# Post-LN transformer layer on eight cores: V jobs moved four blocks, part of the output projection inside head 15, bias on VectorE, one load of constants

## The reference

```
q = (x @ Wq.T + bq) * cos(rot);  k = (x @ Wk.T + bk) * sin(rot);  v = x @ Wv.T + bv     # by head
scores = q @ k.T / sqrt(128) * spiral_weight[head]
attn_out = concat_heads(softmax(scores) @ v) @ Wo.T + bo
x = layernorm(x + attn_out)
h = gelu(x @ proj1.T + proj1_bias)        # 8192 wide, exact gelu
out = layernorm(x + h @ proj2.T + proj2_bias)
```

## Time and profile before

| | |
|---|---|
| median of the runs | 1903.7 us |
| the profiled execution | 1906.13 us outside, its slowest core 2 has a span of 1904.7 us |
| spans of the eight cores | 1893.7 to 1904.7 us, clock 0.987 to 0.991 |
| TensorE busy | 1815.4 us (95%) |
| VectorE, ScalarE, GpSimd busy | 677.6, 555.0, 180.3 us (36%, 29%, 9%) |
| chain that ended last | TensorE 90%, DMA 3%, VectorE 3% |
| first matmul | at 24.3 us, after a wait that ended with the load of `spiral_bc` |
| HBM | 240.32 MB read, 18.87 MB written |

### The profile page before, as it was taken

How to read it: one execution, slowest core, us unless ns; L and a number is a source line. 1 busy time by engine, 2 the same in 40 slices (tenths; PEclk the granted TensorE clock), 3 DMA queues, 4 the chain that set the end, 5 groups by cost and what they waited for, 6 DMA issues and landing times.

```text
span 1904.7 us, 22132 instructions; the slowest of 8 cores (1893.7 to 1904.7 us)
## 1 busy us (share of the span) xinstructions
PE 1815.4 (95%) x8344; PEld 821.9 (43%) x8512; DVE 677.6 (36%) x732; ACT 555.0 (29%) x560; POOL 180.3 (9%) x260
## 2 busy tenths in 40 slices
PE   4999999999999999968899999999999999999998
PEld 1444444444444443323444444444444444444443
DVE  0136666666666667786751000000000020120303
ACT  0145555555555556642332111111110000000002
POOL 2000000000000000050220000000000000000001
PEclk9999999999999999978999999999999999999999
DMA  9661014101411123176344444444443465444665
GB/s 150 112 113 23 15 20 72 23 15 20 67 23 23 23 34 55 23 147 119 133 152 103 75 75 75 77 76 77 78 78 67 80 138 100 97 96 87 154 117 171
DMA packets 46039, 151.59 MB, mean 80 GB/s; under 512 B 6128, under 2 KB 6256, under 8 KB 43632
## 3 DMA queue, kind: packets, MB, share of 16 engines
q0 software_dynamic: 29952, 109.07, 34.1%
q1 hardware_dynamic: 15984, 41.10, 6.4%
HBM read 240.32 MB, written 18.87 MB: 136 GB/s over the span
## 4 chain that ended last, share of the span: by engine, by line
PE 90%; DMA 3%; DVE 3%; DVEq 1%; ACT 1%; issue 1%; POOL 0%; ACTq 0%; POOLq 0%
PE ps L674 22%; PE ps L701 22%; PE ps L381 11%; PE ps L389 11%; PE ps L385 6%; PE ps L569 6%; PE ps L532 5%; PE ps L640 3%; DMA W<-wvc 2%; PE ps L601 1%; DMA H<-p2n 1%; DVE X L924 1%; PE ps L652 1%; PE ps L542 1%; DVEq L927 1%
## 5 line engine op out<-in xcount | busy, mean ns | idle before, releaser
L674 PE MATMUL ps<-X,W 128*128 128x512 bf16 x1945 | 426.3, 379 | 2.1
L701 PE MATMUL ps<-W,H 128*128 128x512 bf16 x1882 | 414.2, 379 | 2.0
L776 ACT ACTIVATE X<-ps,neg_b 128x1024 bf16<-128x1024 f32 x256 | 284.2, 1113 | 303.6 <-PE ps L569 283.5
L928 DVE TENSOR_TENSOR X<-X 128x1024 f32<-128x1024 f32 x224 | 274.4, 1225 | 212.7 <-ACT X L776 202.8
L674 PEld LDWEIGHTS ps<-X,W 128*128 128x128 bf16 x1984 | 194.1, 98 | 234.1
L701 PEld LDWEIGHTS ps<-W,H 128*128 128x128 bf16 x1920 | 188.1, 98 | 227.3 <-issue 1.3
L381 PE MATMUL ps<-H,W 128*128 128x512 bf16 x1007 | 254.2, 380 | 25.2 <-DMA spiral_bc<-spiralr 24.3
L985 DVE TENSOR_TENSOR X<-ps,bo_bc 128x512 f32<-128x512 f32 x24 | 16.4, 685 | 685.9 <-PE ps L701 685.5
L389 PE MATMUL ps<-W,H 128*128 128x512 bf16 x1004 | 246.4, 381 | 3.6 <-DMA W<-wvc 1.8
L532 PE MATMUL ps<-X,H 128*128 128x512 bf16 x496 | 153.8, 390 | 25.6 <-ACT X L776 24.0
L828 ACT ACTIVATE H<-ps,b_sb 128x1024 bf16<-128x1024 f32 x64 | 71.2, 1113 | 360.3 <-PE ps L674 359.2
(11 more groups left out here) (92 smaller groups left out, 856.9 us busy)
## 6 DMA issues: line engine op xcount, KB each, us to landing
W<-p1t POOLq DMA_DIRECT2D x64, 512.0 KB, 5.0
W<-p2n POOLq DMA_DIRECT2D x60, 512.0 KB, 6.7
W<-wkt POOLq DMA_DIRECT2D x16, 512.0 KB, 5.1
H<-xtc POOLq DMA_DIRECT2D x16, 512.0 KB, 50.4
W<-wvc POOLq DMA_DIRECT2D x16, 512.0 KB, 14.6
W<-wqt POOLq DMA_DIRECT2D x16, 512.0 KB, 5.1
H<-won POOLq DMA_DIRECT2D x16, 512.0 KB, 17.3
bo_bc<-x_scr SPq DMA_DIRECT2D x32, 256.0 KB, 6.9
```

The lines of the kernel that those rows point to most:

```text
L674: ins = t.matmul(bank[b0 + c], wslab[ring(ho)][:, half(i, 128)], X[:, i * 1024 + c * 512:i * 1024 + (c + 1) * 512], start=(i == 0), stop=( ...
L701: ins = t.matmul(bank[s], hid[k][:, half(s, 128)], w[:, half(i, 512)], start=(k == 0), stop=(k == 63))
L776: a.activation(out=pbuf[n % 3], in_=pair[turn(h, tc) % 2], func=AF.Exp, bias=neg_b[:, h:h + 1]).then_inc(a_exp, 1)
L928: v.tensor_add(acc, acc, pbuf[n % 3]).then_inc(d_acc, 1)
```

## The change

**V.** The lead-in makes 12 of the 16 V blocks of the first four heads. The last four are jobs of head 0, and each round of later V blocks is made four blocks, that is one head, later. `jobs(12)` goes from 6 to 10.

**Steps.** Heads 13 and 14 (6 jobs) get 8 job matmuls a step instead of 10, and their norms move from step 12 to 13 (squares accordingly).

**Output projection.** The weights of heads 4 to 7 go to the V slabs of W, those of 8 to 15 where x chunks 0 and 1 lay; they load in groups of four in heads 13, 14 and 15. In steps 2 to 15 of head 15, TensorE does two of block 1's matmuls (banks 6 and 7) for heads 0 to 13, ahead of the step's P times V. After the head come banks 4 and 5 of block 1, then block 0.

**Bias.** VectorE adds the output bias, in pieces of 512 columns: three blocks before the projection's first bank, then one block ahead, two pieces after bank 2 and two after the scaling. GpSimd's adds are gone. The xn loads wait for step 8 of head 15 as well. Slabs 2 to 5 of the MLP wait for the end of the projection.

**Constants.** Helix, bq, bk, spiral and pick come in one load of 128 x 72; the two arrays of ones are set by VectorE. TensorE no longer waits for them. The loads of gelu bias, identity, output bias and the second V bias wait for 8 V blocks.

```diff
 def jobs(h):
-    return 10 if h < 12 else 6 if h < 15 else 0
+    return 10 if h < 13 else 6 if h < 15 else 0
+def per_step(h):
+    return 10 if h < 13 else 8
+def norm_step(h):
+    return 12 if h < 13 else 13
...
         def _(e):
-            for dst, src in ((helix_sb, helix2), (bk2_sb, bk2), (bq2_sb, bq2),
-                             (ones_sq_sb, ones_sq), (onesf_sb, onesf),
-                             (pick8_sb, pick8)):
-                e.dma_start(out=dst[:], in_=src[:]).then_inc(s_bias, 16)
-            e.dma_start(out=spiral_bc[:], in_=spiralr.to_broadcast([128, 16]),
-                        ).then_inc(s_bias, 16)
+            e.dma_start(out=consts_sb[:], in_=consts[:]).then_inc(s_bias, 16)
             for c in range(4):
-                if c == 2:
+                if c == 1:
+                    e.wait_ge(d_v, 8)
...
             e.wait_ge(pe_q, 32)
-            for s in (2, 0, 1):
+            e.wait_ge(pe_sc, 248)
+            for s in range(3):
                 e.dma_start(out=xb[s], in_=xn[s * 128:(s + 1) * 128, :]).then_inc(s_xb[s], 16)
...
-                if h % 4 == 0 and h < 12:
-                    e.wait_ge(pe_v, 4 * h + 16)
+                if h % 4 == 1 and h < 12:
+                    e.wait_ge(pe_v, 4 * h + 12)
...
+                if h == 13:
+                    e.wait_ge(pe_v, 64)
+                    for d in range(4, 8):
+                        load(wo_sb[d], won[d], s_wo[d])
+                if h == 14:
+                    e.wait_ge(pe_k, 64)
+                    e.wait_ge(pe_q, 32)
+                    for d in range(8, 12):
+                        load(wo_sb[d], won[d], s_wo[d])
-            e.wait_ge(pe_v, 64)
-            e.wait_ge(pe_q, 32)
-            for d in range(4, 16):
+            for d in range(12, 16):
                 load(wo_sb[d], won[d], s_wo[d])
-
-            def add_bo(s):
-                e.wait_ge(s_xb[s % 3], 16 * (s // 3 + 1))
-                e.tensor_add(xb[s % 3], xb[s % 3], bo_bc[:]).then_inc(g_bo, 1)
...
-            t.wait_ge(s_bias, 112)
...
                 else:
-                    ins = v_mm(4 * (h % 4) + j - 6, i, b)
+                    ins = v_mm((12 + 4 * h + j - 6) % 16, i, b)
...
+                if h % 4 == 0 and tc in (0, 12, 13, 14, 15):
+                    t.wait_ge(d_v, 4 * h + max(12, tc + 1))
...
+                    u = per_step(h) * tc
+                    fill(h, u, u + per_step(h) // 2)
+                    if h == 15 and tc >= 2:
+                        if tc == 2:
+                            t.wait_ge(a_q, 32)
+                        wo_ready(tc - 2)
+                        for c in (2, 3):
+                            wo_mm(1, tc - 2, c)
                     if n > 0:
                         p_v(n - 1)
...
+            def add_bo(s, c):
+                if c == 0:
+                    v.wait_ge(s_xb[s % 3], 16 * (s // 3 + 1))
+                v.tensor_add(xb[s % 3][:, half(c, 512)], xb[s % 3][:, half(c, 512)],
+                             bo_bc[:, half(c, 512)])
+
+            v.wait_ge(s_bo, 16)
+            for s in range(3):
+                for c in range(4):
+                    add_bo(s, c)
+            v.drain()
             for s in range(8):
-                v.wait_ge(g_bo, s + 1)
                 for c in range(4):
...
+                    if c == 2 and 2 <= s < 7:
+                        add_bo(s + 1, 0)
+                        add_bo(s + 1, 1)
...
+                if 2 <= s < 7:
+                    add_bo(s + 1, 2)
+                    add_bo(s + 1, 3)
+                    v.drain()
```

More of the change, by code:

```diff
@@ L545, in denom, with wo_ready, wo_mm @@
                 ins.then_inc(pe_den, 1)
+            def wo_ready(d):
+                t.wait_ge(s_wo[d], 16)
+                t.wait_ge(d_norm, d + 1)
+            def wo_mm(s, d, c):
+                ins = t.matmul(bank[s * 4 + c], pool_a[d][:, half(s, 128)],
+                               wo_sb[d][:, half(c, 512)], start=(d == 0), stop=(d == 15))
+                if d == 15:
+                    ins.then_inc(pe_wo, 1)
             for h in range(16):
@@ L596, in transposes @@
                     ins.then_inc(pe_tr, 1)
[L600 to L616 removed]
+            t.wait_ge(a_av, 16)
+            for d in range(8):
+                for c in (0, 1):
+                    wo_mm(1, d, c)
+            t.wait_ge(a_exp, 255)
+            denom(15, pair[(turn(15, 15) + 1) % 2])
+            for d in range(8, 14):
+                for c in (0, 1):
+                    wo_mm(1, d, c)
             t.wait_ge(a_exp, 256)
             t.wait_ge(a_den, 16)
[L619 removed]
+            for d in range(14):
                 for c in range(4):
                     wo_mm(0, d, c)
[L622 to L624 removed]
+            for d in range(14, 16):
+                wo_ready(d)
                 for s in range(2):
@@ L906, in normalise @@
                 v.tensor_mul(pool_a[h], avraw, rec).then_inc(d_norm, 1)
[L908 to L909 removed]
+            for m in range(11):
+                v_out(m, ((2, 3, 4, 5), (0, 2, 3, 1), (5, 4, 4))[m // 4][m % 4])
             norm_pick(0, pair[1])
[L911 removed]
+            v_out(11, 5)
             norm_out(0, pair[1])
[L913 removed]
             for h in range(16):
@@ L932, in _ @@
                         normalise(h - 1)
+                    for j in range(6, jobs(h)):
+                        if tc == (16 * j + 15) // per_step(h):
+                            v_out(6 + 4 * h + j, 6 + j % 2)
                     if tc == 15:
@@ L937, in _ @@
                         v.tensor_sub(hl[:, half(1)], acc, hl[:, half(0)]).then_inc(d_hl, 1)
-                    for j in range(6, jobs(h)):
-                        if tc == (16 * j + 15) // PER_STEP:
-                            v_out(10 + 4 * h + j, 6 + j % 2)
             for i in range(4):
```

187 lines of the change are left out of this document (71 added, 116 removed).

## The result

| | before | after |
|---|---|---|
| runs | 1903.53 us median (1903.34 to 1904.17) | 1877.07 and 1878.39 us |
| profiled execution | 1906.13 us | 1877.07 us |
| span of its slowest core | 1904.7 us (core 2) | 1875.4 us (core 4) |
| spans of all cores | 1893.7 to 1904.7 us | 1866.5 to 1875.4 us |
| TensorE busy | 1815.4 us (95%) | 1809.8 us (97%) |

The ratio is 0.9864, 95% interval 0.984 to 0.9888: 25.9 us less; the forecast, 1870 against 1903.7, was 33.7. Two more runs of the changed kernel fell in a disturbed state with a lower clock (2167 and 2179 us) and are left out, so its time rests on two runs.

A forecast was written before the change was run, and what follows sets the result against it. TensorE, busy in 95% of the span, was taken as the bound. Terms -3.0 + 0.6 - 9.1 - 14.0 - 4.9 - 3.0 = -33.4 took the profiled 1906.1 us to 1872.7, as median 1870; range 1861 to 1881.

The forecast's parts named there:

- A, start: Start of the lead-in: fewer small loads land the last V piece 4.2 us earlier, slow clock costs 1.2; -3.0 us.
- A2, lead-in: Lead-in: loads issued after 8 V blocks cost 0 (bounds 0 to +4.4), with 3.2 us slack for the third K chunk.
- rival 2: Start gains nothing and takes some: broadcasts ahead of x cost +4.4 us, 1875, or 1878 with the slow clock; 12%.
- A3, norm of head 0: End of lead-in: without the 16th V block, head 0's norm is no longer hidden; +0.6 us (0 to 1.2).
- B, V: Four V blocks leave the lead-in (-13.8 us), heads 12 to 14 grow by 4.7; -9.1 us (-13.4 to -5.1).
- C, head 15: Head 15: VectorE's chain without its stall cuts 41.3 us to 27.3, including +1.9 for slow clock; -14.0 (-15.9 to -10).
- Rival 1: Head 15: DMA traffic, not GpSimd, stalls VectorE, so the head's gain shrinks to nothing: 1884 us; 3%.
- D, first projection: Output projection of the first two blocks: 28 matmuls less (-6.0), +0.4 and +1.0 in waits; -4.9 us (-5.9 to -3).
- E, blocks 2 to 7: Projection blocks 2 to 7: no stretched VectorE scalings, the transposes' 3.4 us of waits go; -3.0 us (-3.4 to +2).
- Rival 3: TensorE leaves head 15 at 1.2 GHz and stays there through the projection: up to +104 us, 1975; 2%.
- Rival 4: Weights for head 15's projection matmuls come up to 6 us late and stop TensorE: 1876 us; 5%.
- The 2.4 us to the median: The median of the runs lies 2.4 us below the profiled execution, so the forecast goes from 1872.7 to 1870.

The follow-up runs named there:

- the start alone: Kernel before with one load of constants, memsets, no TensorE wait, identity and gelu bias after 8 V blocks, output bias after 16: ratio 0.9973.
- the best version: Changed kernel with later output-bias load, ScalarE copying block 0's transposes earlier, head 14's reciprocals and normalise behind head 15's sums, GpSimd adding blocks 1-2's bias: 1863.84 us.

## Why the prediction was right, and where not

The time (1877.7 by the ratio, 1877.07 and 1878.39 by its runs) lies in the range of 1861 to 1881 but 7.7 us above the forecast of 1870: the gain was 25.9 us, not 33.4. By parts, from the experiments: -15.6 (bias) - 5.1 (start) - 3.4 (V) - 5.9 (matmuls in head 15) = -30.0, and +3.8 for the output bias that is issued after 8 V blocks, which none of the single parts contains (the start alone issued it after 16). That gives -26.2 against -25.9 measured. So close an agreement is luck, since each part is uncertain by 2 to 5 us; the means of the cores give -25.2 against -26.3. That the early broadcast costs only with V moved is argued, not shown: no run has it without that move. On the means the misses are 2.0 us up to the first scores, 2.9 in heads 12 to 14 and 2.3 in the projection; head 15 came out as forecast (-14.1).

- **A, start: right place, one term wrong.** "Removing that wait is not worth 24 us" is confirmed: it is worth 0. I took -3.0; the mean core gained 4.3 us, the slowest 6.6. The 4.2 us for the small loads was nearly right: on the mean of the eight cores the last V piece starts at 40.4 us before, at 36.1 with the start alone and at 35.6 in the changed kernel. What was wrong is the 1.2 us for the lower level: the last piece's 16 matmuls ran at full rate on all eight cores (3.61 or 3.62 us), and the slow ones were earlier (5.64 us at 16.61), where a wait followed anyway. So the cold start cost 0. The rule of the Trainium skill, "TensorE: Matmul & The Clock Gate", section "HAM oscillation — how this bites in real kernels", which I had weighed at 3.45 us on that piece, did not hold for it; the wait in front of it was 1.75 us, and the waits of the page's example are longer, so this says nothing against the page. In other runs it did happen on single cores, at no cost to the last piece: with the start alone, on core 6, the third piece took 5.30 us behind a wait of 2.12.
- **A2, lead-in: wrong, and the largest miss.** I worked out a slack of 3.2 us and let the broadcast come "mostly behind x". It came beside it: 4.03 us of wait. With the slow matmuls after it, that is rival 2, whose +4.4 was about right (3.8 by the runs; 3.2 in the first scores on the mean core, 5.1 on the last). I gave it 12%. Its own rows spoke for it: 1.3 MB issued at 69 us while x was due at 77 to 80.
- **A3, norm of head 0: right place, cost not there.** First scores follow the norm at once. The first exponent is not waited for: the norm is written at 93.87 us on core 4, and P times V starts at 95.65 without a wait, 4.1 us of matmuls behind the first scores where I had counted 3.0. The +0.6 was 0.
- **B, V: the lead-in part right, the idle time wrong.** Head 12 took 49.25 us, as forecast (49 to 50). Heads 13 and 14 idled 6.3 and 7.0 us; I took 4.5 and 6.0, believing that smaller steps would fill the idle time. Three settings (8, 10 and 12 a step) say that they do not: the norm's waits stay. B was -6.3 in the trace instead of -9.1, and -3.4 by the runs with V alone (interval -5.7 to -1.3). The term that failed is the idle time of heads 13 and 14: I had it shrink from 14.5 us together to 10.5, and it was 13.3.
- **C, head 15: right in cause and nearly in size.** -14.8 against -14.0. Rival 1, that the transfers stall VectorE, is dead: DMA at 1.03 in a window with no stretched sum, and 0.83 in one with eight. The +1.9 for the clock was not needed; with the 28 matmuls in the head it stayed at 1.00. That VectorE then sets the head's length was right, and the best version lives on it.
- **D, first projection: right.** -5.6 against -4.9; my own three terms add up to -4.6. The +1.0 at the third block did not come, its wait stayed at 2.2 us. The twelve adds took 7.30 us instead of 8.4, back to back.
- **E, blocks 2 to 7: half.** The transposes wait for nothing, as forecast, but the next matmul does, 2.49 us, for ScalarE, which copied block 0's transposes only after it had waited for block 1's rows. I had asked what delays the transposes and not what takes their result away. Moving those copies, with two other moves, gave 3.4 us.
- **Rival 3** (TensorE stays at 1.2 GHz) did not come: granted clock 1.00 in the first projection and 0.98 in blocks 2 to 7. **Rival 4** (weights late) did not come: no wait at the projection matmuls in head 15.
- **The 2.4 us to the median** was an assumption that two medians lie equally far under their profiled executions. The changed kernel's profiled execution lay at its runs (1877.07 of 1877.07 and 1878.39). Against the profiled executions alone the change was -29.1, against the medians -25.9; 3.2 us of my miss are in no term of the sum. Most of them fit with summing on one late core: in the profile before, its MLP starts 5.0 us behind the mean of the eight, in the one after 2.4.

Open: why the profiled execution of before is 2.4 us above its median, and why the projection gained 7.6 us on the slowest cores but 5.6 on the mean. Cores differ by such amounts in one execution (the first scores of before spread over 4.9 us).

## What to carry to other kernels

An elementwise engine's idle time is not a place to put work if its neighbour on the same memory is on the critical path: three adds of 4.5 us on GpSimd, with the five later ones, cost 15.6 us, and the first three blocks' adds stood in VectorE's own idle time for nothing. A long wait at the start of a load-bound stretch is worth what is still missing at its end, so look at the last operand to land before the first wait. When work is removed from a lead-in, everything behind it is wanted earlier, so the loads that were put "late enough" must be counted again, and with the new date. And a change of some microseconds is not read from the slowest core of one trace against the slowest of another: the mean over all cores agreed with the runs where the slowest cores were up to 3 us off.

## What the runs showed of the hardware that was not expected

- GpSimd's adds hold up VectorE's two-input operations by about their own time, wherever they fall: +14.7 us on the one sum beside 13.5 us of adds before, where the sum ends 1.1 us behind the last add, and +12.4 on eight beside 14.2 us of them with the bias back on GpSimd. It does not take a large operation: one on 128 x 1 elements that takes 0.16 us elsewhere stood 4.25 us behind an add. And it goes both ways: an add that starts 0.2 us behind a scaling took 5.55 us instead of 4.5. Both in the kernel before:

```profile
945.01 4.50 POOL L343 TENSOR_TENSOR W<-W,bo_bc 128x2048 f32<-128x2048 f32 x1 [4.96 <-DMA W<-xn]
945.28 4.25 DVE L957 SCALAR_TENSOR_TENSOR ln_nm<-ln_mv,ln_rs 128x1 f32<-128x1 f32 x1
...
962.09 1.34 DVE L962 TENSOR_SCALAR H<-H,ln_rs,ln_nm 128x2048 bf16<-128x2048 f32 x1
962.29 5.55 POOL L343 TENSOR_TENSOR H<-H,bo_bc 128x2048 f32<-128x2048 f32 x1 [12.78 <-DMA H<-xn]
```

What they did not touch were reciprocals: two GpSimd adds beside them left four at 6.58 and 6.57 us. The normalising product between them, with two inputs, took 1.52 us instead of 1.23, where an add's last 0.44 us lay beside it. The Trainium skill, "SBUF — State Buffer", section "SBUF: two separate sides", says that the two engines take a shared port pair by an exclusive lock, that whichever starts first keeps it for its whole instruction, and that of VectorE's operations those with two SBUF inputs or in a two-port mode need it. The rows above agree, with one exception: the sum of 15.89 us is shown to start 1.3 us ahead of the first add. Why it was held all the same stays open.
- The scaling that took 5.53 us before takes 1.34 or 1.35 us in every block after. It has one input tile and two columns of scalars. It is no single case: on cores 1, 3 and 7 of the same profile one scaling took 5.59, 5.41 and 5.37 us, each within 0.22 us of the start of an add, and with the add at 962.29 above it was the add that was held. So it takes part in the exclusion; by which mode no run shows.
- Matmuls that cost no time raised the clock: head 15 had 0.75 without the 28 and 1.00 with them, at the same length.
- A wait in a dense stretch can leave the matmuls behind it slow, and the length of the wait alone does not say whether. On core 4 of the changed kernel the 20 matmuls behind the 4.03 us wait for x took 1.86 + 5.45 us instead of 1.03 + 3.62, 2.7 us on top of the wait. At the same place the eight cores waited from 1.52 to 4.09 us: behind waits of 2.24, 3.46, 3.75, 4.03 and 4.09 us the next 16 V matmuls took 4.61 to 5.45 us, behind waits of 1.52, 2.32 and 3.16 us they took 3.62. With the output bias later all eight cores waited under 1 us, and none was slow (3.62). The 2.49 us wait in the projection also left some slow (1.43 + 1.91 us for eight matmuls, instead of 2.06).
